# An eight-block fp32 kernel: one layer norm is spread among the parts of a product, gated products go in halves, and GpSimd takes copies and two of eight blocks

## The chip, the cores and the metric

One core of a Trainium2 chip runs the whole program in one launch. TensorE (PE) multiplies matrices into the eight banks of PSUM, VectorE (DVE) and ScalarE (ACT) read PSUM and SBUF, GpSimd (POOL) works on SBUF, SyncE (SP) issues most DMAs. The metric is device microseconds of one execution; the time before is the median of three runs.

## The reference, cut to what matters

The tensor x has 32 images of 16 x 16 points with 32 channels; read as tokens it is 32 sequences of 256. Eight residual blocks follow each other. The change is at the seam between the second (a spectral filter over tokens, "STU") and the third (a triangle product over the grid):

```
t = t + stu(ln(t))                       # spectral filter, by Fourier transform and short lags
n = ln_c(x)                              # the norm of the triangle block
a = sigmoid((n @ Wa1 + ba1) * (n @ Wa2 + ba2))
b = sigmoid((n @ Wb1 + bb1) * (n @ Wb2 + bb2))
g = sigmoid(n @ Wg + bg)
z = einsum('bikc,bkjc->bijc', a, b)      # 16 channels in a and b
x = x + g * (ln(z) @ Wz + bz)
```

## The kernel before, in words

All is float32, and every matmul shows as two instructions in the trace. The order of the work on each engine is written out by hand, with counting semaphores (`S(name)`, `wait_ge`, `then_inc`) between the engines; each engine works its own list strictly in order.

The tokens are kept in four quarters of 64. The late half of the tokens gets the filter's result by frequency products and a way back (`frequencies`, `way_back`, L889), and is ready first (`x_stu` at 1). The second quarter has a frequency product of its own on banks 4 to 7 (128 products of 64 x 32 weights), DVE turns it (`turn_products`, four transposes, L1644), PE takes it back (`way_back` on y_f2) and DVE adds it to quarter 1 (L1659). Quarter 0 gets its result as columns (`stu_cols`, added at L1656).

The norm of the triangle block (`LN_TRI`) goes quarter by quarter in the order 2, 3, 0, 1 (`TRI_ORDER`): PE subtracts the mean (`ln_centre`, L271), ACT squares (L370), PE spreads the mean square (`ln_spread`, L277), ACT takes Ln (L376) and Exp (L381), DVE multiplies (`normalise`, L1665). Before, DVE writes that product twice (`twice`): as columns `xm` in the arena, from which PE makes b and the gate, and as rows `xnH` (in the storage of xR), from which PE makes a.

Then PE makes the columns of a (`a_columns`) and of b, DVE adds the bias (`add_ab_bias`, L1681) and multiplies the two projections (L1695), and ACT takes the sigmoid (L1359 for a, L1371 for b). The matrix `a_bd` holds a eight times, each copy times a mask (`par16`): three blocks on ACT (`blocks_of_a`, L1362), five on DVE (L1700). When `a_bd` and `b_s` are there, PE makes z (L962). Most plain matmuls go through the helper `full`, L665, `keep_busy` among them: products whose result nobody reads.

Of the kernel before, what the change touches and what calls it, by code (L numbers as in the profile page):

```python
# [42 lines left out]
BUSY = {2: 2, 3: 6, 4: 1, 5: 1, 7: 0}  # L43
BUSY_ATTN, BUSY_TRI, BUSY_SCAN, BUSY_LOGITS = 4, (2, 2, 3, 1), 3, 2
BUSY_ROW, BUSY_START, BUSY_BACK = 1, 3, 1
# [3 lines left out]
BUSY_DRAIN = 1  # L49
ACT_BD, ACT_BD_FIRST = 3, 2  # L50
RES = 8
# [52 lines left out]
def build(nc, force_steps=False, **d):  # L104
    x, out = d["x"], d["out"]
    with ExitStack() as ctx:
# [155 lines left out]
        def var_bank(i):  # L262
            return [2, 4, 6, 4, 6, 6, 6, 6, 6][norm_of(i)] + i % 2

# [330 lines left out]
        def _(pool):  # L595
# [38 lines left out]


            def add_states(i):
                pool.wait_ge(S("x_early"), RES * (i + 1))
                pool.wait_ge(S("verdict"), i + 1)
                by_steps = pool.value_load(unsettled[0:1, i:i + 1], min_val=0, max_val=1)
                with pool.If(by_steps != 0):  # L640
                    pool.wait_ge(S("y_final"), i + 1)
                    for r in range(RES):
                        pool.tensor_tensor(*state_sum(i, r), ALU.add).then_inc(S(f"x_again{i}"), 1)
                        pool.wait_ge(S(f"x_again{i}"), r + 1)
# [16 lines left out]
        def _(pe):  # L661
# [212 lines left out]

            def frequencies(k0, rows, w):
                y_ps = bank[:, k0:k0 + 4, :].rearrange("p k n -> p (k n)")
                for n in range(FREQ // NQ):
                    for k in range(NQ):
                        f = FREQ // NQ * k + n
                        last = full(y_ps[C * k:C * k + C, 2 * C * n:2 * C * n + 2 * C], x_fb[rows, f, :],  # L880
                                    w[rows, f // FI, f % FI, :, :])
                last.then_inc(S("y_f_ps"), 1)

# [21 lines left out]

            pe.wait_ge(S("stu_rows"), 1)
            frequencies(4, slice(0, 2 * C), w_fr[1])

            pe.wait_ge(S("x_stu"), 1)
            for r in range(NQ):  # L910
                for q in range(NQ):
                    last = full(bank[C * q:C * q + C, 0, r * P:(r + 1) * P], ident[:, C * r:C * r + C],
                                r_stu.rearrange("p (n b) -> p n b", b=B)[:, :, G * q:G * q + G])
            last.then_inc(S("stu_cols"), 1)

            def centre_tri(p):
                pe.wait_ge(S("x_stu"), max(1, p))
                ln_centre(pe, ln_at(LN_TRI) + p, tokens(xQ, TRI_ORDER[p]))

            centre_tri(0)  # L920
            centre_tri(1)
            pe.wait_ge(S("y_f"), 8)
            way_back(y_f2, 0, range(G), 1, slice(T // 4, T // 2))
            ln_spread(pe, ln_at(LN_TRI))
            centre_tri(2)
            ln_spread(pe, ln_at(LN_TRI) + 1)

            def a_columns(ms):
                for m in ms:
# [3 lines left out]
                    if m % 8 == 7:  # L933
                        last.then_inc(S("ab_ps"), 1)

            pe.wait_ge(S("w_late_in"), 16)
            centre_tri(3)
            a_columns(range(8, 12))
            ln_spread(pe, ln_at(LN_TRI) + 2)
            a_columns(range(12, 16))  # L940
            ln_spread(pe, ln_at(LN_TRI) + 3)
            a_columns(range(0, 4))
            keep_busy(BUSY_TRI[0], 6)
            a_columns(range(4, 8))
            for m in range(16):
                last = full(bank[:, 4 + m // 4, (m % 4) * P:(m % 4 + 1) * P], xm[:, m * P:(m + 1) * P], wb)
# [7 lines left out]
            keep_busy(BUSY_TRI[1], 6)  # L954
            pe.wait_ge(S("a_bd"), 2)
            pe.wait_ge(S("b_s"), 1)
# [232 lines left out]
        def _(act):  # L1189
# [155 lines left out]
            ln_square(act, tri + 1)  # L1345
            ln_rstd(act, tri)
            ln_square(act, tri + 2)
            ln_rstd(act, tri + 1)
            ln_square(act, tri + 3)
            ln_rstd(act, tri + 2)  # L1350
            ln_rstd(act, tri + 3)
# [5 lines left out]
            sigmoids()  # L1357
            act.wait_ge(S("a_in"), 1)
            act.activation(a_s[:, :], a_in[:, :].rearrange("p (h m) -> p m h", h=16), ACT.Sigmoid).then_inc(S("a_s"), 1)  # L1359
            def blocks_of_a(gs):  # L1360
# [5 lines left out]
            act.wait_ge(S("a_s"), 1)  # L1366
            blocks_of_a(range(ACT_BD_FIRST))
            act.wait_ge(S("b_in"), 1)
# [4 lines left out]
            last.then_inc(S("b_s"), 1)  # L1373
            blocks_of_a(range(ACT_BD_FIRST, ACT_BD)).then_inc(S("a_bd"), 1)
            act.wait_ge(S("gate_ps"), 1)
# [118 lines left out]
        def _(dve):  # L1494
# [152 lines left out]
            for half in range(2):  # L1647
# [3 lines left out]
            last.then_inc(S("x_stu"), 1)  # L1651
            turn_products(1, y_f2)

            dve.wait_ge(S("stu_cols"), 1)
            x0 = tokens(xQ, 0).rearrange("p g (n r) -> p g n r", r=NQ)
            dve.tensor_tensor(x0, bank[:, 0, :].rearrange("p (r n g) -> p g n r", r=NQ, g=G), x0, ALU.add)\  # L1656
                .then_inc(S("x_stu"), 1)
            dve.wait_ge(S("back_f"), 3)
            dve.tensor_tensor(tokens(xQ, 1), by_batch(bank[:, 1, :]), tokens(xQ, 1), ALU.add).then_inc(S("x_stu"), 1)  # L1659

            def twice(j, i):

                h4 = xnH[:, 4 * j:4 * j + 4, :, :].rearrange("p h g w -> p g h w")
                for out_ in (xm.rearrange("p (w g h) -> p g h w", w=W, g=G)[:, :, 4 * j:4 * j + 4, :], h4):
                    last = dve.tensor_tensor(out_, bank[:, j, :].rearrange("p (g h w) -> p g h w", g=G, w=W),  # L1665
                                             rs[:, i % 2, :].rearrange("p (g h w) -> p g h w", g=G, w=W), ALU.mult)
                last.then_inc(S("ln_applied"), 1)

            def normalise(p):
                dve.wait_ge(S("ln_rstd"), ln_at(LN_TRI) + p + 1)  # L1670
                twice(TRI_ORDER[p], ln_at(LN_TRI) + p)

            normalise(0)
            normalise(1)
            normalise(2)
            pre4 = ab_pre.rearrange("p (m n) -> p m n", n=2 * CT)

            def add_ab_bias(k, half):
# [4 lines left out]
                                         ab_bias[:, k:k + 1, :].to_broadcast([P, 32, 2 * CT]), ALU.add)  # L1683

            dve.wait_ge(S("w_late_in"), 16)
            link(add_ab_bias(0, 1))
            normalise(3)
            for k in range(2):
                if k:
                    dve.wait_ge(S("a_in"), 1)  # L1690
                    link(add_ab_bias(1, 0))
                last = add_ab_bias(k, k)
                last.then_inc(S(["a_pre", "b_pre"][k]), 1)
                dve.wait_ge(S(["a_pre", "b_pre"][k]), 1)
                dve.tensor_tensor((b_in if k else a_in).rearrange("p (m c) -> p m c", c=CT), pre4[:, :, 0:CT], pre4[:, :, CT:2 * CT],  # L1695
                                  ALU.mult).then_inc(S(["a_in", "b_in"][k]), 1)

            dve.wait_ge(S("a_s"), 1)
            for g in range(ACT_BD, 8):
                last = dve.tensor_scalar(a_bd[:, :, g, :], a_s.rearrange("p (m i) -> p m i", i=16),  # L1700
# [333 lines left out]
```

## Time and profile before

| what | value |
|---|---|
| median of three runs | 379.24 us (376.47, 379.24, 379.54) |
| profiled execution, its own time | 377.4 us |
| span of its trace, first to last instruction | 374.0 us |
| mean granted TensorE clock | 0.989 of full speed |
| busy: PE, DVE, ACT, POOL | 341.5, 228.9, 190.7, 35.5 us |

The span is what the trace covers; 3.4 us of the execution's own time lie around it. Busy times of the engines overlap. A timeline row gives the start of an instruction or of several merged ones, the time from the first's start to the last's end, and in brackets how long the engine had been idle and what released it. "x256" counts instructions, two for each float32 matmul.

### The profile page before, as it was taken

To read this page: it belongs to the slowest core of one execution; us is meant where nothing else is said; L and a number is where in the kernel's file an instruction comes from. 1 tells how busy PE (TensorE), PEld (TensorE's weight loads), DVE (VectorE), ACT (ScalarE), POOL (GpSimd) and SP (SyncE) were. 2 spreads that over 40 slices of the span, in tenths; PEclk is the share of its full clock that TensorE was granted. 3 is DMA by queue.
4 is the path that set the end of the run, shared out by engine and by line. 5 is a ranking of instruction groups with operands and counts; after the bars stand their busy time and mean duration, and the time that the engine had idled before them with its cause. 6 is when DMAs were issued, how large, how long until landed. Compare 5 with 4: busy or idle time off the path is not lost.

```text
span 374.0 us, 9464 instructions
## 1 busy us (share of the span) xinstructions
PE 341.5 (91%) x4044; PEld 228.4 (61%) x4044; DVE 228.9 (61%) x461; ACT 190.7 (51%) x415; POOL 35.5 (9%) x38
## 2 busy tenths in 40 slices
PE   7969999999998999998889999799998899999890
PEld 2545666566646899956556379257646554773790
DVE  5679768689848403156956764643446476245894
ACT  2988688988868300044862656530346215033460
POOL 4027512122210001000000000000000000000000
PEclk9999999999999999999999999999999899999997
DMA  8960000000070000020000000000000000000004
GB/s 232 127 197 1 2 4 2 2 4 2 3 169 3 4 4 2 4 59 2 0 2 2 0 3 0 4 0 2 2 0 2 0 3 0 2 2 1 0 2 115
DMA packets 7426, 8.95 MB, mean 24 GB/s; under 512 B 3840, under 2 KB 6544, under 8 KB 7056
## 3 DMA queue, kind: packets, MB, share of 16 engines
q1 hardware_dynamic: 5718, 7.28, 9.1%
q10 hardware_dynamic: 1664, 1.05, 0.9%
q8 instruction: 33, 0.54, 0.6%
q14 instruction: 11, 0.09, 0.1%
HBM read 5.70 MB, written 1.05 MB: 18 GB/s over the span
## 4 chain that ended last, share of the span: by engine, by line
PE 64%; DVE 14%; ACT 10%; issue 5%; DMA 4%; SPq 2%; DVEq 0%; ACTq 0%
PE bank L665 30%; PE bank L1098 6%; PE bank L277 5%; PE bank L271 4%; DMA arena<-in_w_spec 4%; PE bank L1025 4%; PE bank L1036 3%; PE bank L865 2%; PE bank L889 2%; ACT lnv L376 2%; SPq L561 1%; ACT rs L381 1%; DVE arena L1796 1%; PE bank L778 1%; PE bank L1155 1%
## 5 line engine op out<-in xcount | busy, mean ns | idle before, releaser
L370 ACT ACTIVATE sq<-bank 128x512 f32<-128x512 f32 x33 | 19.4, 591 | 64.1 <-PE bank L271 50.4
L665 PE MATMUL bank<-xn,sb_w_attn 128*128 128x512 f32 x64 | 34.5, 621 | 3.7 <-ACT attn_scratch L1233 1.9
L665 PE MATMUL bank<-sb_consts 128*128 128x512 f32 (+1 forms) x80 | 35.4, 553 | 0.0
L277 PE MATMUL bank<-sq,sb_consts 128*128 128x512 f32 x66 | 34.7, 611 | 0.5 <-ACT sq L370 0.2
L376 ACT ACTIVATE lnv<-bank 128x512 f32<-128x512 f32 x33 | 19.7, 596 | 30.2 <-PE bank L277 29.9
L1098 PEld LDWEIGHTS bank<-arena,sb_w_late 128*128 128x128 f32 x180 | 23.0, 190 | 10.9 <-DVE arena L1854 8.0
L665 PE MATMUL bank<-arena 64*32 64x256 f32 (+4 forms) x466 | 26.6, 381 | 2.5 <-ACT arena L1266 1.2
L1098 PE MATMUL bank<-arena,sb_w_late 128*128 128x128 f32 (+1 forms) x180 | 26.4, 283 | 1.5 <-DVE arena L1854 0.3
L611 POOL TENSOR_TENSOR attn_scratch<-attn_scratch 128x512 f32<-128x512 f32 x16 | 20.4, 1275 | 72.1 <-DVE attn_scratch L1567 72.1
L1036 PE MATMUL bank<-arena,sb_w_late 128*128 128x128 f32 x136 | 26.3, 277 | 0.0
L1025 PE MATMUL bank<-arena,sb_consts 128*128 128x128 f32 x136 | 26.1, 276 | 0.1
L665 PEld LDWEIGHTS bank<-arena 64*32 64x32 f32 (+3 forms) x466 | 17.2, 167 | 14.5 <-issue 6.7
L1406 ACT ACTIVATE arena<-bank 128x128 f32<-128x128 f32 x68 | 18.8, 277 | 13.3 <-PE bank L1036 13.1
L665 PE MATMUL bank<-arena,attn_scratch 128*32 128x128 f32 (+2 forms) x768 | 23.9, 293 | 0.6 <-DVE attn_scratch L1609 0.6
L1854 DVE SCALAR_TENSOR_TENSOR arena<-bank,xn 128x128 f32<-128x128 f32 x30 | 8.7, 290 | 25.5 <-PE bank L1098 25.1
L665 PEld LDWEIGHTS bank<-arena,attn_scratch 128*32 128x32 f32 (+1 forms) x768 | 22.7, 129 | 1.9 <-DVE attn_scratch L1609 0.8
L271 PE MATMUL bank<-xQ,sb_consts 128*128 128x512 f32 x40 | 20.9, 613 | 1.0 <-DMA sb_consts<-in_consts 0.6
L1025 PEld LDWEIGHTS bank<-arena,sb_consts 128*128 128x128 f32 x136 | 20.5, 192 | 1.7 <-issue 1.7
L381 ACT ACTIVATE rs<-lnv 128x512 f32<-128x512 f32 x33 | 20.8, 630 | 1.0
L1036 PEld LDWEIGHTS bank<-arena,sb_w_late 128*128 128x128 f32 x136 | 20.6, 192 | 0.2
L665 PEld LDWEIGHTS bank<-sb_consts 128*128 128x128 f32 x80 | 14.2, 197 | 10.8 <-issue 10.6
L665 PEld LDWEIGHTS bank<-wvo,xn 128*128 128x128 f32 x128 | 15.9, 191 | 6.2 <-issue 6.2
(208 smaller groups left out, 625.3 us busy)
## 6 DMA issues: line engine op xcount, KB each, us to landing
sb_w_late<-in_w_late SPq DMA_DIRECT2D x1, 1100.5 KB, 18.6
arena<-in_w_spec SPq DMA_DIRECT2D x4, 256.0 KB
arena<-arena SPq DMA_DIRECT2D x4, 256.0 KB, 4.1
arena<-fourier SPq DMA_DIRECT2D x1, 768.0 KB, 16.4
sb_w_attn<-in_w_attn SPq DMA_DIRECT2D x1, 641.0 KB, 8.2
xR<-in_x ACTq DMA_DIRECT2D x4, 128.0 KB, 3.1
xR<-in_x SPq DMA_DIRECT2D x4, 128.0 KB, 4.1
arena<-arena SPq DMA_DIRECT2D x4, 128.0 KB, 2.3
```

Of the source, the lines that this page charges most:

```text
L271: pe.matmul(bank[:, centre_bank(i), :], centre, src, start=True, stop=True).then_inc(S("ln_centred"), 1)
L277: pe.matmul(bank[:, var_bank(i), :], mean32, sq[:, i % 2, :], start=True, stop=True)\
L370: act.activation(sq[:, i % 2, :], bank[:, centre_bank(i), :], ACT.Square).then_inc(S("ln_squared"), 1)
L376: act.activation(lnv[:, i % 2, :], bank[:, var_bank(i), :], ACT.Ln, bias=LN_EPS[norm_of(i)])\
L381: act.activation(rs[:, i % 2, :], lnv[:, i % 2, :], ACT.Exp, scale=-0.5).then_inc(S("ln_rstd"), 1)
L611: link(pool.tensor_tensor(qn[:, u % QN, :], qe[:, u % 2, :], qn[:, u % QN, :], ALU.mult))
L665: return mm(ps, lhsT, rhs, start=True, stop=True)
L1025: mm(place(s, h), ident, z_[:, h, s % RES, :, :], start=True, stop=False)
L1036: mm(place(s_, h), rvt[i], before(h, s_ % RES), start=False, stop=True)\
L1098: last = mm(bank[:, 4 + h % 2, B * lo:B * hi], band[i][:, w, :], carry[:, h - 1, w + lo:w + hi, :], start=(w == 1), stop=(w == 2), skip_gr ...
L1406: act.activation(y_[:, h, s_ % RES, 1:PASS + 1, :], bank[:, 4 + h + 2 * (s_ % 2), 0:PASS * HALF].rearrange("p (n g) -> p n g", g=HALF), AC ...
L1854: dve.scalar_tensor_tensor(out=carry[:, h, 1:5, :], in0=bank[:, 4 + h % 2, 0:P].rearrange("p (w b) -> p w b", b=B), scalar=0.0, in1=xn[:, ...
```

## The change

PE: the second quarter's 128 frequency products are cut into four parts; the centring and spreading of quarters 2 and 3, and the product for quarter 0's columns, stand between the parts. The way back of the second quarter comes after the columns of a for quarters 2 and 3, in bank 6 and no longer in bank 1. The spread of the norm uses banks 1, 0, 1, 4. One of two idle products ahead of the last columns of a is dropped. The products for b wait for POOL's copies.

DVE: quarters 2 and 3 are normalised ahead of the transposes, once each (rows only). The gated products of a and b are made in halves. DVE makes four of the eight blocks of `a_bd`.

POOL: copies each normalised quarter from rows to columns, and makes two blocks of `a_bd`.

ACT: the square of quarter 0 comes after the Exp of quarter 3; the sigmoid of a goes in two halves; two blocks of `a_bd` in place of three, both ahead of the sigmoid of b.

```diff
-BUSY_ATTN, BUSY_TRI, BUSY_SCAN, BUSY_LOGITS = 4, (2, 2, 3, 1), 3, 2
+BUSY_ATTN, BUSY_TRI, BUSY_SCAN, BUSY_LOGITS = 4, (1, 2, 3, 1), 3, 2
...
-ACT_BD, ACT_BD_FIRST = 3, 2
+ACT_BD, POOL_BD = 2, 2
...
         def var_bank(i):
-            return [2, 4, 6, 4, 6, 6, 6, 6, 6][norm_of(i)] + i % 2
+            k = norm_of(i)
+            if k == LN_TRI:
+                return [1, 0, 1, 4][i - ln_at(k)]
+            return [2, 4, 6, None, 6, 6, 6, 6, 6][k] + i % 2
...
# gpsimd, behind the zeroing of b_s
+            for p in range(CH):
+                rows = slice(4 * TRI_ORDER[p], 4 * TRI_ORDER[p] + 4)
+                pool.wait_ge(S("ln_applied"), ln_at(LN_TRI) + p + 1)
+                pool.tensor_copy(xm.rearrange("p (w g h) -> p g h w", w=W, g=G)[:, :, rows, :],
+                                 xnH[:, rows, :, :].rearrange("p h g w -> p g h w")).then_inc(S("xm_in"), 1)
+            pool.wait_ge(S("a_s"), 1)
+            for g in range(8 - POOL_BD, 8):
+                last = pool.tensor_scalar(a_bd[:, :, g, :], a_s.rearrange("p (m i) -> p m i", i=16), par16[:, g:g + 1],
+                                          None, ALU.mult)
+            last.then_inc(S("a_bd"), 1)
...
# tensor
             pe.wait_ge(S("stu_rows"), 1)
-            frequencies(4, slice(0, 2 * C), w_fr[1])
-            ...                               # stu_cols, as in stu_columns() below
-            centre_tri(0)
-            centre_tri(1)
-            pe.wait_ge(S("y_f"), 8)
-            way_back(y_f2, 0, range(G), 1, slice(T // 4, T // 2))
-            ln_spread(pe, ln_at(LN_TRI))
-            centre_tri(2)
-            ln_spread(pe, ln_at(LN_TRI) + 1)
+            second_quarter(0)
+            centre_tri(0)
+            centre_tri(1)
+            second_quarter(1)
+            ln_spread(pe, ln_at(LN_TRI))
+            ln_spread(pe, ln_at(LN_TRI) + 1)
+            second_quarter(2)
+            stu_columns()                     # waits for ln_logged of quarter 3
+            second_quarter(3)
+            centre_tri(2)
             pe.wait_ge(S("w_late_in"), 16)
-            centre_tri(3)
             a_columns(range(8, 12))
             ln_spread(pe, ln_at(LN_TRI) + 2)
             a_columns(range(12, 16))
+            pe.wait_ge(S("y_f"), 8)
+            way_back(y_f2, 0, range(G), 6, slice(T // 4, T // 2))
+            pe.wait_ge(S("ln_logged"), ln_at(LN_TRI) + 3)
+            centre_tri(3)
+            a_columns(range(0, 2))
             ln_spread(pe, ln_at(LN_TRI) + 3)
-            a_columns(range(0, 4))
+            a_columns(range(2, 4))
             keep_busy(BUSY_TRI[0], 6)
             a_columns(range(4, 8))
+            pe.wait_ge(S("xm_in"), CH)
             for m in range(16):
...
-            pe.wait_ge(S("a_bd"), 2)
+            pe.wait_ge(S("a_bd"), 3)
...
# scalar
+            for half in (1, 0):
+                act.wait_ge(S("a_in"), 2 - half)
+                last = act.activation(a_s.rearrange("p (m h) -> p m h", h=16)[:, :, 8 * half:8 * half + 8],
+                                      a_in[:, 512 * half:512 * half + 512].rearrange("p (h m) -> p m h", h=8), ACT.Sigmoid)
+            last.then_inc(S("a_s"), 1)
...
# vector
-            turn_products(1, y_f2)
+            normalise(0)                      # rows only
+            normalise(1)
             dve.wait_ge(S("stu_cols"), 1)
...
+            turn_products(1, y_f2)
...
             link(add_ab_bias(0, 1))
+            ab_product(0, 1).then_inc(S("a_in"), 1)
+            normalise(2)
+            dve.wait_ge(S("back_f"), 3)
+            dve.tensor_tensor(tokens(xQ, 1), by_batch(bank[:, 6, :]), tokens(xQ, 1), ALU.add).then_inc(S("x_stu"), 1)
             normalise(3)
+            add_ab_bias(0, 0).then_inc(S("a_pre"), 1)
+            dve.wait_ge(S("a_pre"), 1)
+            ab_product(0, 0).then_inc(S("a_in"), 1)
+            dve.wait_ge(S("a_in"), 2)
+            link(add_ab_bias(1, 0))
+            ab_product(1, 0)
+            add_ab_bias(1, 1).then_inc(S("b_pre"), 1)
+            dve.wait_ge(S("b_pre"), 1)
+            ab_product(1, 1).then_inc(S("b_in"), 1)

             dve.wait_ge(S("a_s"), 1)
-            for g in range(ACT_BD, 8):
+            for g in range(ACT_BD, 8 - POOL_BD):
```

## Rows read from the trace of the kernel before

**Rows 1.** Windows: stretch, length, busy PE, PEld, DVE, ACT, POOL, granted clock, DMA share, GB/s.

```profile
150.00:165.00 15.00, 15.00 (x423) 12.81 (x424) 4.47 (x7) 1.21 (x2) 0.00 (x0) 1.00 0.02 4
165.00:176.00 11.00, 9.46 (x42) 5.16 (x41) 7.36 (x9) 7.13 (x11) 0.00 (x0) 1.00 0.24 48
```

**Rows 2.** Timeline, 149 to 167 us: start, length, instruction, [idle before <-releaser].

```profile
149.87 8.17 PE L665 MATMUL bank<-arena,attn_scratch 64*32 64x64 f32 x256
150.00 0.69 DVE L1650 TENSOR_TENSOR xQ<-bank,xQ 128x512 f32<-128x512 f32 x1 [1.06 <-PE bank L889]
...
158.98 1.98 PE L271 MATMUL bank<-xQ,sb_consts 128*128 128x512 f32 x4
...
160.90 3.10 PE L889 MATMUL bank<-arena,attn_scratch 128*32 128x64 f32 x128
...
163.93 1.13 PE L277 MATMUL bank<-sq,sb_consts 128*128 128x512 f32 x2
164.05 1.21 SPq L561 DMA_DIRECT2D arena<-in_w  x3
164.06 0.69 DVE L1659 TENSOR_TENSOR xQ<-bank,xQ 128x512 f32<-128x512 f32 x1 [2.84 <-PE bank L889]
...
165.09 0.60 ACT L376 ACTIVATE lnv<-bank 128x512 f32<-128x512 f32 x1 [3.48 <-PE bank L277]
...
165.72 0.63 ACT L381 ACTIVATE rs<-lnv 128x512 f32<-128x512 f32 x1
```

**Rows 3.** Timeline, 175 to 188 us.

```profile
175.66 1.16 PE L665 MATMUL bank<-sb_w_late,xR 128*128 128x128 f32 x8
...
176.66 3.74 PE L665 MATMUL bank<-sb_w_late,arena 128*128 128x128 f32 x32
176.86 1.22 DVE L1681 TENSOR_TENSOR arena<-bank,sb_w_late 128x1024 f32<-128x1024 f32 x1 [1.25 <-PE bank L665]
...
179.38 2.02 ACT L1359 ACTIVATE arena<-arena 128x1024 f32<-128x1024 f32 x1 [5.01 <-DVE arena L1695]
...
180.23 3.60 PE L665 MATMUL bank<-arena,sb_w_late 128*128 128x512 f32 x8
...
181.43 2.19 ACT L1362 ACTIVATE arena<-arena,sb_consts 128x1024 f32<-128x1024 f32 x2
...
181.89 1.23 DVE L1695 TENSOR_TENSOR arena<-arena 128x1024 f32<-128x1024 f32 x1
...
183.03 3.40 DVE L1700 TENSOR_SCALAR arena<-arena,sb_consts 128x1024 f32<-128x1024 f32 x5
...
183.52 2.11 ACT L1371 ACTIVATE arena<-arena 128x512 f32<-128x512 f32 x2
...
186.73 3.77 PE L962 MATMUL bank<-arena 128*32 128x128 f32 x128 [1.18 <-ACT arena L1362]
```

**Rows 4.** Groups by line and shape, DVE, 145 to 200 us: busy us, mean ns.

```profile
L1665 DVE TENSOR_TENSOR arena<-bank,rs 128x512 f32<-128x512 f32 x4 | 4.2, 1040 | 3.5 <-ACT rs L381 3.5
...
L1665 DVE TENSOR_TENSOR xR<-bank,rs 128x512 f32<-128x512 f32 x4 | 2.7, 671 | 0.0
L1644 DVE STREAM_TRANSPOSE attn_scratch<-bank 128x512 f32<-128x512 f32 x4 | 2.5, 684 | 7.4 <-PE bank L665 7.4
```

**Rows 5.** Groups by line and shape, POOL, whole span.

```profile
L611 POOL TENSOR_TENSOR attn_scratch<-attn_scratch 128x512 f32<-128x512 f32 x16 | 20.4, 1275 | 72.1 <-DVE attn_scratch L1567 72.1
L625 POOL TENSOR_TENSOR arena<-arena 128x1024 f32<-128x1024 f32 x3 | 7.1, 2361 | 0.5 <-POOL attn_scratch L611 0.5
...
L619 POOL TENSOR_SCALAR sb_w_stu<-sb_w_stu,sig 128x128 f32<-128x128 f32 x1 | 0.6, 620 | 0.2 <-POOL attn_scratch L611 0.2
```

**Rows 6.** Timeline, 1.7 to 5.8 us, POOL and DVE.

```profile
1.74 3.52 POOL L607 MEMSET arena<- 128x4096 f32 x1 [0.15 <-POOL arena L605]
...
4.54 0.73 DVE L1511 TENSOR_SCALAR fw<-fw 128x4 f32<-128x4 f32 x1
...
5.51 0.23 DVE L1513 TENSOR_SCALAR fw<-fw 128x4 f32<-128x4 f32 x1
```

## What the change is predicted to do

> **What bounds the kernel now.** After the page I read the chain of waits through the seam between the filter and the triangle block, then the windows there, then the timeline row by row. The windows say that the seam has two halves of different kind. From 150 to 165 us PE is busy all the time, at the full 2.4 GHz level (granted clock 1.00) [rows 1]: it works through the second quarter's product, the first centrings and the way back without a hole [rows 2]. From 165 us on no engine is full (PE 9.46, DVE 7.36, ACT 7.13 of 11 us) [rows 1]: here the end is set by a relay, and its last part is what the reader should follow [rows 3]: last columns of a (175.66), bias on DVE (176.86), product, sigmoid on ACT (179.38 to 181.40), two blocks of a_bd, sigmoid of b, a third block on ACT, and only then z on PE at 186.73, released by that third ACT block. What the change is worth is how much earlier z starts; behind z nothing is edited, so that difference goes to the end undiminished.
>
> **The front: what moves.** The second quarter's 256 instructions take 8.17 us [rows 2], 2.04 for each of the four parts, from 149.87. The add that the centring waits for ends at 150.69 [rows 2], so nothing waits at 151.9, and PE stays the bound. I add up PE's list. Four instructions of centring take 1.98 with the tail, some 0.43 each in the stream; the product and the columns of quarter 0 together end where centring starts, 9.11 after 149.87, so the columns cost about 1.0 [rows 2]. Eight instructions of a's columns cost 1.00 (176.66 - 175.66) [rows 3]. The way back costs 3.03 (163.93 - 160.90) [rows 2]. Cutting the product makes PE go five more times from one shape of weights to another; I take 0.1 for each, worked out from that 1.0 for 32 short instructions, bounds 0 and 0.3. Sum: 149.87 + 8.17 + four products of 0.86 + 1.0 + 0.96 (centre quarter 0) + 1.0 + 0.96 + 1.0 + 3.03 + 0.5 = 170.0 for the end of the way back, which was 163.93.
>
> Covered on the way, at nothing: squares, Ln and Exp of quarters 2 and 3, finished at about 160 beside the third part of the product (Ln starts 1.16 after its spread, Ln and Exp take 1.26 [rows 2]); the products for quarter 0's columns wait for that Ln, which is about 0.8 us early; behind that new wait on PE stand the fourth part and all the rest. The transposes (2.5 [rows 4]) run from 163.1 to 165.7 and are due at 166.9. DVE's half bias, half product and normalise(2) end at about 169.7, due at 170.1: the thinnest cover, and if it is gone each tenth goes to the end. The SP queue waits for back_f at 3, so its three loads of the expert weights leave at about 170 and not at 164.05 [rows 2]; the experts are two layers on, which is time enough.
>
> Behind the way back the relay of quarter 1: add 0.69, centre and square, spread, Ln and Exp 1.26, normalise 0.67 [rows 2, 4]. With the lags of the rows: add 170.13 to 170.82, square 172.04 to 172.63, spread 172.7, Ln 173.84, Exp to 175.10, normalise to 175.80, last columns of a at 175.85. Before they started at 175.66 [rows 3]. **So the front, for all its moving, gives -0.2 to +0.3: nothing.** What it took away (four writes of 1.04 us into the columns, on DVE [rows 4]) was on the path, and the longer PE list takes its place.
>
> **The back: what gets shorter.** Bias at 177.05 (the same lag of 1.20), 1.22 long; the product of one half, about 0.65 (half of 1.23, and some start); the sigmoid of one half, about 1.1 (half of 2.02, and some start) [rows 3]: a_s at 180.1 and not 181.40. Gain here 1.3.
> On b: POOL's fourth copy starts at 175.85. The trace shows no such copy; bounds are 0.5 (a memset at 3.52 per 4096 elements [rows 6] has only writes) and 1.28 (two inputs, 512 elements [rows 5]), with up to half as much again for the scattered write, as DVE shows (1.04 against 0.67 [rows 4]). I take 0.8, near the memset: at most one read. It ends at 176.7, PE's a columns at 176.85, so it is hidden; at 2.0 it would cost 1.0. Products for b 176.85 to 180.42, the gate's and the idle ones to 185.8 (3.57, 3.60 and 1.8 by instruction count [rows 3]).
> DVE: bias of b 179.0 to 180.2, product half to 180.9, bias to 182.15, product half to 182.85 (183.12 before). ACT: two blocks 180.1 to 182.3, sigmoid of b 182.9 to 185.0, and no third block. DVE: four blocks of 0.68 (3.40/5 [rows 3]).
> POOL: two blocks of 1024 elements behind a_s. Nearest rows: 0.62 for a tensor_scalar of 128 elements, and two-input tensor_tensors of 1.28 and 2.36 for 512 and 1024, 2.12 ns an element [rows 5]. A memset's 0.86 ns an element [rows 6] and one input of two (1.06 ns) give 1.4 and 1.6 for a block; the 128-element row scaled by 8 gives 5.0. I take 1.5: POOL from 180.2 to 183.2.
>
> **Where the two meet.** One early pair of rows decides how I let POOL and DVE overlap: a DVE tensor_scalar of four elements, which takes 0.23 alone, takes 0.73 when it starts inside POOL's long memset, and ends at 5.27, 0.01 after the memset's end at 5.26 [rows 6]. So DVE's blocks, which are tensor_scalars at 0.66 ns an element (the tensor_tensor of as many needs 1.20 [rows 3]), will not run beside POOL's: they wait from 182.85 to 183.2 and end at 185.9. z starts at 186.0, with PE itself ready at 185.8. **Sum: 186.73 - 186.0 = 0.7 us saved.** Without that meeting z would start at PE's 185.8.
> The Trainium skill (SBUF — State Buffer, Who interferes with whom) calls this an exclusive lock on a port pair that DVE's two-port modes share with GpSimd, and the trace agrees for tensor_scalar (0.73 against 0.23). The same section goes further and says that a DVE instruction with two SBUF inputs also contends with a GpSimd one that reads SBUF; no row here shows or denies that, and it would turn the sign of the sum: the second rival.
>
> **The rivals.** (1) POOL and DVE don't disturb each other in these shapes, and POOL is quick: z at PE's 185.8, a gain of 0.9 to 1.0. For it: only one instruction shows the wait. Against: it shows it to 0.01 us.
> (2) Slower: the half products of b (two SBUF inputs) also wait for POOL's blocks, and POOL's for them. Place: 180.2, where POOL begins and the first half product is ready at nearly the same time. Then everything with the port stands in one line: block 180.2 to 181.7, product to 182.35, block to 183.85 (the second bias beside it), product to 184.5, four blocks to 187.2, z at 187.3: 0.55 later than before. It decides from POOL blocks of about 1.2 us up; each 0.1 on a block costs 0.2, so 2.36 would make it 2.3 us.
> (3) POOL's block is far dearer than 1.5: at 5.0 POOL ends at 190.2, DVE's blocks at 192.9, z 6.2 late. The 128-element row allows it, the longer rows speak against it.
> (4) PE's clock falls in a new hole. PE would idle 1.2 us at most here; before, it stood 1.18 us ahead of z [rows 3] and kept 1.00.
> That the change doesn't do what it says has little room: each moved step has its own wait.
>
> **How the numbers follow.** The profiled execution took 377.4 us on its own clock, so the forecast by its rows is 376.7; rival 1 gives 376.4, rival 2 377.95 (to 379.7), rival 3 up to 383.6. The runs shown are 376.47, 377.4, 379.24 and 379.54: the profiled one is 1.8 below the median, and four draws spread over 3 us, so about 1% is what a measurement of this kernel can tell from no change. The new time will be such a draw; I set the sum on the mean of the four, 378.2: 377.5 for the forecast, 377.2 to 377.3 for rival 1, 378.7 for rival 2. Chances: forecast 0.38, rival 2 0.32, rival 1 0.18, rival 3 in some degree 0.08, the clock 0.04. Range: rival 1 with a low draw (2 below) 375.0; rival 2 with a high draw (1.5 above) 380.3. Faster by over 1% has no case but a misread front, 0.04; slower by over 1% needs rival 3 at its full size or the clock, 0.06; within 1% 0.90.
>
> **What would show each step.** Last columns of a at 175.5 to 176.2 (front right); the end of the half sigmoid near 180.1; xm copies under 1.0 and never the last release of b's products; POOL's blocks near 1.5 with b's two half products at 0.65 (forecast) or with a start or length drawn out to a POOL block's end (rival 2); the first of DVE's four blocks ending later than 0.7 after its start (the meeting); z released by DVE, near 186.0. The prediction is wrong if the spread of quarter 1 or the copies release PE much later than this, if POOL's blocks pass 2 us, or if the clock in 165 to 190 is not 1.00.

## The result, and the profile after

The changed kernel took 380.91 us in the median (378.76 to 384.19), the kernel before 379.11 beside it: a ratio of 1.0059, 95% interval 1.0038 to 1.0079. A second set of the same kernel gave 1.0028 (1.0004 to 1.0051). So it is slower, by 0.3 to 0.6%, where 377.5 us, 0.7 less than the mean of the runs then known, was forecast. The profiled execution took 380.7 us, 3.3 more than that of before. Its page:

```profile
span 377.8 us, 9462 instructions
PE 344.9 (91%) x4042; PEld 229.8 (61%) x4042; DVE 227.5 (60%) x458; ACT 190.3 (50%) x415; POOL 46.4 (12%) x44
```

DVE lost 1.4 us, POOL gained 10.9. What matters is the seam, in the timeline of after:

```profile
149.09 2.17 PE L680 MATMUL bank<-arena,attn_scratch 64*32 64x64 f32 x64
...
169.30 0.69 DVE L1717 TENSOR_TENSOR xQ<-bank,xQ 128x512 f32<-128x512 f32 x1 [0.46 <-PE bank L905]
...
175.12 1.16 PE L680 MATMUL bank<-sb_w_late,xR 128*128 128x128 f32 x8 [0.77 <-DVE xR L1686]
175.13 1.09 POOL L642 COPY arena<-xR 128x512 f32<-128x512 f32 x1 [5.17 <-DVE xR L1686]
...
176.26 3.65 PEld L680 LDWEIGHTS bank<-sb_w_late,arena 128*128 128x128 f32 x32 [0.18 <-POOL arena L642]
...
178.30 1.11 ACT L1388 ACTIVATE arena<-arena 128x512 f32<-128x512 f32 x1 [1.54 <-DVE arena L1709]
179.51 6.54 POOL L646 TENSOR_SCALAR arena<-arena,sb_consts 128x1024 f32<-128x1024 f32 x2 [3.30 <-ACT arena L1388]
179.68 1.49 DVE L1709 TENSOR_TENSOR arena<-arena 128x512 f32<-128x512 f32 x1
...
182.34 0.72 DVE L1709 TENSOR_TENSOR arena<-arena 128x512 f32<-128x512 f32 x1
182.98 4.27 DVE L1731 TENSOR_SCALAR arena<-arena,sb_consts 128x1024 f32<-128x1024 f32 x4
...
187.31 5.44 PE L990 MATMUL bank<-arena 128*32 128x128 f32 x128 [2.06 <-DVE arena L1731]
```

The second quarter's product (t0) begins between 149.0 and 151.5 in the profiles of this study, at 149.87 before [rows 2], and nothing ahead of it was edited; so every time of the seam is counted from t0. The reader sees three things. The last columns of a start 26.03 behind t0, before 25.79 [rows 3]: the front gave nothing. The second half of a's sigmoid ends at 179.41, 30.32 behind t0, before 31.53: the halves paid 1.2. Then that is lost again and more: POOL's two blocks take 6.54, beside them DVE's first half product takes 1.49 and its four blocks 4.27, and z starts 38.22 behind t0 and not 36.86 [rows 2, 3]: **1.36 us late**, 0.36% of the time. Here z also took 5.44 for 3.77. The windows (columns: stretch, length, PE, PEld, DVE, ACT, POOL busy with counts, granted clock, DMA share, GB/s) say why:

```profile
186.00:187.00 1.00, 0.00 (x0) 0.00 (x0) 1.00 (x2) 1.00 (x1) 0.06 (x1) 1.00 0.00 0
187.00:188.00 1.00, 0.69 (x20) 0.66 (x24) 0.26 (x1) 0.06 (x1) 0.00 (x0) 0.83 0.00 0
188.00:189.00 1.00, 1.00 (x26) 0.96 (x25) 0.00 (x0) 0.00 (x0) 0.00 (x0) 0.50 0.00 0
...
190.00:191.00 1.00, 1.00 (x28) 0.96 (x23) 0.00 (x0) 0.22 (x1) 0.00 (x0) 0.50 0.00 0
191.00:192.00 1.00, 1.00 (x42) 1.00 (x37) 0.00 (x0) 0.98 (x2) 0.00 (x0) 0.97 0.06 16
```

PE had idled 2.06 us (a hole of 2.06, in what follows), and the granted clock went to 0.50, the 1.2 GHz level, for some 3 us. At the end of z the profiled execution is -0.78 (t0) + 1.36 + 1.67 = 2.25 behind that of before. A further 1.0 comes between z's end and a late centring (338.83 before, 342.08 after), a stretch in which the clock read 0.95 from 225 to 260 us and 1.00 before. The single profiles of the kernels below show 0.95 or 1.00 in that stretch, 0.95 also in the fastest; I don't lay it on the change.

### The profile page after: what moved, and what is told of

It is laid out like the page before. It is cut to its first block, busy times and chain, and to the rows that moved or that the text cites. A ratio compares the mean times of both kernels' runs of the same rounds, so it can differ in the third digit from the quotient of the medians.

```text
span 377.8 us, 9462 instructions
## 1 busy us (share of the span) xinstructions
PE 344.9 (91%) x4042; PEld 229.8 (61%) x4042; DVE 227.5 (60%) x458; ACT 190.3 (50%) x415; POOL 46.4 (12%) x44
## 4 chain that ended last, share of the span: by engine, by line
PE 69%; DVE 16%; ACT 9%; issue 4%; DMA 1%; SPq 0%; DVEq 0%; ACTq 0%
PE bank L680 31%; PE bank L280 7%; PE bank L1126 6%; PE bank L274 6%; PE bank L1053 4%; PE bank L1064 3%; PE bank L880 2%; PE bank L905 2%; ACT lnv L379 2%; PE bank L990 1%; ACT rs L384 1%; DMA sb_consts<-in_consts 1%; DVE arena L1827 1%; PE bank L781 1%; DVE arena L1731 1%
## 5 line engine op out<-in xcount | busy, mean ns | idle before, releaser
L1126 PEld LDWEIGHTS bank<-arena,sb_w_late 128*128 128x128 f32 x180 | 23.0, 190 | 10.9 <-DVE arena L1885 8.0
L665 POOL MEMSET arena<- 128x128 f32 x4 | 0.8, 206 | 155.3 <-DVE xQ L1873 131.8
```

The costliest lines, as they stand in the source:

```text
L1126: last = mm(bank[:, 4 + h % 2, B * lo:B * hi], band[i][:, w, :], carry[:, h - 1, w + lo:w + hi, :], start=(w == 1), stop=(w == 2), skip_gr ...
```

## The experiments

After the result I held one theory, that POOL's two blocks, by their own length and by what they do to DVE, make z late; and one rival, that the clock's fall behind the hole ahead of z is the loss. Later a third question came up: where the gain of the copies went. No kernel leaves any of the computation out. Ratios are to the kernel before on the same chip, with 95% intervals; "z" is its start counted from the t0 of the same trace.

| kernel | t0, us | z from t0, us | z long, us | ratio |
|---|---|---|---|---|
| before | 149.87 | 36.86 | 3.77 | |
| the changed kernel | 149.09 | 38.22 | 5.44 | 1.0059 (1.0038 to 1.0079) |
| the same again (e12) | 150.81 | 38.21 | 3.77 | 1.0028 (1.0004 to 1.0051) |
| e1: no POOL blocks, six on DVE | 150.28 | 37.13 | 3.77 | 1.0028 (1.0003 to 1.0052) |
| e3: one POOL block | 149.49 | 37.29 | 3.77 | 1.0006 (0.9983 to 1.0029) |
| e9: no POOL blocks, ACT three | 150.74 | 36.52 | 3.77 | 0.9992 (0.9965 to 1.0018) |
| e10: e9 with DVE's columns | 151.45 | 37.66 | 3.77 | 1.0027 (0.9996 to 1.0057) |
| e5: POOL's blocks kept apart | 150.21 | 41.51 | 3.77 | profiled only, 384.05 us |
| e2: hole filled | 151.21 | 38.17 | 3.77 | 1.0016 (0.9994 to 1.0037) |
| e4: before with POOL's blocks | 149.11 | 38.16 | 3.77 | 1.0076 (1.0049 to 1.0104) |
| e7: e4, hole filled | 149.04 | 38.16 | 3.77 | 0.9988 (0.9971 to 1.0004) |
| e8: before, one idle product more | 151.01 | 36.87 | 3.77 | 1.0017 (0.9993 to 1.0041) |
| e6: before with the halves | 151.29 | 36.18 | 3.77 | 0.9970 (0.9953 to 0.9986) |
| e11: e6 with POOL's copies | 149.10 | 34.32 | 3.77 | 0.9900 (0.9869 to 0.9932) |

**e1_no_pool_blocks.** The changed kernel without POOL's blocks; DVE makes six.

```diff
-ACT_BD, POOL_BD = 2, 2
+ACT_BD, POOL_BD = 2, 0
-            pool.wait_ge(S("a_s"), 1)      # and the loop of two tensor_scalars
-            pe.wait_ge(S("a_bd"), 3)
+            pe.wait_ge(S("a_bd"), 2)
```

> The changed kernel without POOL's two blocks: POOL still copies the columns, DVE makes six blocks. Theory A (POOL's two blocks are the loss: 2.85 and 3.72 us long, they draw out DVE's product to 1.49 and its four blocks to 4.27, and the hole that this leaves on PE lets the clock fall in z): the product takes 0.69, six blocks about 4.1, z starts 37.2 to 37.4 us after the second quarter's product and not 38.2, the granted clock in z is 1.00 and z takes 3.8: 2.5 us below the changed kernel, so within 0.5 us of the kernel before. Rival C (the loss is in the new order of the norm and in POOL's copies): it stays 1.5 us or more above the kernel before.

z came at 37.13, 1.09 earlier than with POOL's blocks. Its timeline:

```profile
180.83 0.69 DVE L1704 TENSOR_TENSOR arena<-arena 128x512 f32<-128x512 f32 x1
...
183.30 4.06 DVE L1726 TENSOR_SCALAR arena<-arena,sb_consts 128x1024 f32<-128x1024 f32 x6
187.41 3.77 PE L985 MATMUL bank<-arena 128*32 128x128 f32 x128 [1.01 <-DVE arena L1726]
```

Without POOL beside it DVE's half product takes 0.69 for 1.49, and six blocks take 4.06, less than four took (4.27). The ratio did not follow as far as z did: by z it should be 1.0007, its interval begins at 1.0003 and its middle is 1.0028, which the second set of the changed kernel has too. So the time expected here, within 0.5 us of the kernel before, was missed. The span of the trace is on record for every execution: in the mean it is 1.56 us longer than that of the kernel before, of which z is 0.27 and the granted clock, 0.0019 lower, by the estimate given under e12 some 0.6; 0.7 stays open. That POOL's blocks make z late is shown; that the whole time comes back without them is not.

**e3_one_pool_block.** One block on POOL, five on DVE.

```diff
-ACT_BD, POOL_BD = 2, 2
+ACT_BD, POOL_BD = 2, 1
```

> The changed kernel with one block on POOL and five on DVE. Theory A with a wait that lasts only while POOL has a block: POOL is done at about 33.4 us after the second quarter's product, ahead of DVE's blocks, which take 3.4; the first half product still takes 1.49; z starts at 37.4 to 37.7, with the clock at 1.00: 2 to 2.5 below the changed kernel. If POOL's block costs by its length alone, the same; if what counts is that POOL runs beside DVE at all, half of the 1.36 us by which z is late stays.

```profile
179.90 2.85 POOL L646 TENSOR_SCALAR arena<-arena,sb_consts 128x1024 f32<-128x1024 f32 x1 [3.30 <-ACT arena L1388]
180.07 1.49 DVE L1709 TENSOR_TENSOR arena<-arena 128x512 f32<-128x512 f32 x1
...
183.33 3.40 DVE L1731 TENSOR_SCALAR arena<-arena,sb_consts 128x1024 f32<-128x1024 f32 x5
186.78 3.77 PE L990 MATMUL bank<-arena 128*32 128x128 f32 x128 [1.14 <-DVE arena L1731]
```

The first block still draws the half product out to 1.49, by 0.80. POOL has ended (182.75) when DVE's blocks begin, and five of them take 3.40, as they did before [rows 3]. So the second block costs 0.93 (38.22 - 37.29), nearly all of it on DVE's blocks (4.27 - 3.40).

**e5_pool_alone.** POOL's blocks end before DVE's products of b begin, so each is seen by itself.

```diff
-            last.then_inc(S("a_bd"), 1)      # POOL
+            last.then_inc(S("pool_bd"), 1)
...
             link(add_ab_bias(1, 0))
+            dve.wait_ge(S("pool_bd"), 1)
             ab_product(1, 0)
```

> The changed kernel, but DVE waits with b's first half product, and so with all behind it, until POOL's two blocks are done: their length with nothing on DVE beside them. If POOL's block is dear by itself (the sum's 1.5 was mis-sized): both blocks 2.8 to 2.9, together 5.7, and b's half products 0.69. If the wait for DVE makes them dear: 2.0 to 2.1 each or less (0.8 us less than 2.85, the time by which DVE's product was drawn out). z starts about 4 us later than in the changed kernel either way.

By line (durations in ns: least, median, most), first the kernel after, then e5:

```profile
L646 POOL TENSOR_SCALAR arena<-arena,sb_consts x2: 2851/3284/3717, 179.5 to 182.3; 128x1024 f32<-128x1024 f32 x2
L1731 DVE TENSOR_SCALAR arena<-arena,sb_consts x4: 734/1126/1520, 183.0 to 186.5; 128x1024 f32<-128x1024 f32 x4
```

```profile
L646 POOL TENSOR_SCALAR arena<-arena,sb_consts x2: 2844/2847/2850, 180.6 to 183.4; 128x1024 f32<-128x1024 f32 x2
```

And the timeline of e5:

```profile
186.40 0.69 DVE L1710 TENSOR_TENSOR arena<-arena 128x512 f32<-128x512 f32 x1 [5.63 <-POOL arena L646]
188.28 3.51 PE L680 MATMUL bank<-sb_consts 128*128 128x512 f32 x4 [3.63 <-DVE arena L1704]
188.87 2.74 DVE L1733 TENSOR_SCALAR arena<-arena,sb_consts 128x1024 f32<-128x1024 f32 x4
191.72 3.77 PE L991 MATMUL bank<-arena 128*32 128x128 f32 x128
```

Alone, a POOL block is 2.85 us and four DVE blocks are 2.74. Beside each other POOL's second block is 3.72 and DVE's four 4.27, in turn 1.52, 0.74, 1.51, 0.73. None of DVE's waits until POOL's instruction ends (186.05 in the kernel after). POOL's first block kept its 2.85 and drew out the half product that began 0.17 after it. The second half product, which began together with POOL's second block at 182.34, took only 0.72; there the POOL block grew, beside this product and DVE's first three blocks. What decides which side pays was not tried. The idle products show the clock again: four instructions in 3.51 behind a hole of 3.63, with the granted clock at 0.50 from 188 to 191 us, and in 1.88 elsewhere.

**e2_hole_filled.** Two more idle products ahead of z in the changed kernel; everything else stays.

```diff
-BUSY_ATTN, BUSY_TRI, BUSY_SCAN, BUSY_LOGITS = 4, (1, 2, 3, 1), 3, 2
+BUSY_ATTN, BUSY_TRI, BUSY_SCAN, BUSY_LOGITS = 4, (1, 4, 3, 1), 3, 2
```

> The changed kernel with four idle products in place of two ahead of z, 1.7 us more of them, which end before z can start. Theory A: z still starts at 38.2 us after the second quarter's product, but the granted clock stays 1.00 and z takes 3.8 in place of 5.4: 1.7 us below the changed kernel, 0.3 to 1.0 above the kernel before. Rival B (the clock falls for another reason than the 2.06 us hole ahead of z): z takes 5.4 as before and the time is that of the changed kernel, 2.2 above the kernel before.

```profile
185.44 3.60 PE L680 MATMUL bank<-sb_consts 128*128 128x512 f32 x8
...
189.38 3.77 PE L990 MATMUL bank<-arena 128*32 128x128 f32 x128 [0.34 <-DVE arena L1731]
```

The hole is 0.34, z is 3.77 long and as late as ever (38.17). The ratio is 1.0016: z's late start alone would make 1.0035. What is missing does not lie at the seam, as e7 shows.

**e4_before_pool_blocks.** The kernel before, with POOL making two of DVE's five blocks and nothing else of the change.

```diff
+            pool.wait_ge(S("a_s"), 1)
+            for g in range(8 - POOL_BD, 8):
+                last = pool.tensor_scalar(a_bd[:, :, g, :], a_s.rearrange("p (m i) -> p m i", i=16), par16[:, g:g + 1],
+                                          None, ALU.mult)
+            last.then_inc(S("a_bd"), 1)
...
-            for g in range(ACT_BD, 8):
+            for g in range(ACT_BD, 8 - POOL_BD):
```

> The kernel before with only one part of the change: POOL makes two of DVE's five blocks. Theory A: POOL runs from 31.6 us after the second quarter's product to 37.5 or later and releases z at 37.6 to 38.3 in place of 36.86; the hole on PE ahead of z is over 2 us, the clock falls and z takes over 5 us: 1.5 to 3 us above the kernel before. Rival C: no loss, within 0.5 us of the kernel before.

```profile
180.75 6.46 POOL L637 TENSOR_SCALAR arena<-arena,sb_consts 128x1024 f32<-128x1024 f32 x2 [34.06 <-ACT arena L1364]
181.14 1.79 DVE L1700 TENSOR_TENSOR arena<-arena 128x1024 f32<-128x1024 f32 x1
182.86 3.46 DVE L1705 TENSOR_SCALAR arena<-arena,sb_consts 128x1024 f32<-128x1024 f32 x3
187.27 3.77 PE L967 MATMUL bank<-arena 128*32 128x128 f32 x128 [2.47 <-POOL arena L637]
```

This one edit, that should unload DVE, makes z 1.30 later, with POOL itself the last to come. The product of full size is drawn out from 1.23 [rows 3] to 1.79, three blocks take what five took. The hole of 2.47 left the clock at 1.00 in the profiled execution, where I had expected z at over 5 us: such a hole need not make it fall. The ratio, 1.0076, is 2.9 us, of which z explains 1.30.

**e7_before_pool_blocks_filled** and **e8_before_filled** ask what filling that hole is worth, and whether one more idle product does anything for the kernel before, which has a hole of 1.18 [rows 3].

```diff
# e7: e4 with
+BUSY_ATTN, BUSY_TRI, BUSY_SCAN, BUSY_LOGITS = 4, (2, 4, 3, 1), 3, 2
# e8: before with
+BUSY_ATTN, BUSY_TRI, BUSY_SCAN, BUSY_LOGITS = 4, (2, 3, 3, 1), 3, 2
```

> The kernel before with POOL's two blocks, and four idle products in place of two ahead of z. That kernel without the fill was 2.9 us above before, of which 1.3 is z's later start, though in the one profiled execution the clock stayed 1.00 behind a hole of 2.47 us. If the rest is the clock falling in many of the timed executions: z starts at 38.2 as without the fill and the time falls to 1.0 to 1.8 above before. If the rest has another cause: it stays at 2.5 to 3.3.

> The kernel before with three idle products in place of two ahead of z, which end at about 36.4, ahead of z at 36.86: a control for the fill. If the fill helps only where the hole is long: the same time as before, within 0.5 us. If the clock falls in the kernel before too in some executions, or if idle products help anywhere: 0.5 to 1.5 us below.

```profile
187.20 3.77 PE L967 MATMUL bank<-arena 128*32 128x128 f32 x128 [0.74 <-POOL arena L637]
```

e7 has z where e4 has it (38.16, hole 0.74), and measures 0.9988 against 1.0076; e8 measures 1.0017, no gain. That e7 comes out no slower than before, with z 1.3 us later, has its reason outside the seam. In the mean e7's span is 1.18 us longer than that of the kernel before beside it, which agrees with z's 1.30; but only 1.84 us of its time lie outside the span, against 3.65. e2 is the same case: its span is 2.36 longer, with 1.82 outside against 3.62, and its mean span, 377.44, lies between those of the two sets of the changed kernel, 378.15 and 377.24. e8 has 1.61 outside, and its span is 2.67 longer without any delay of z; the clock, 0.0034 lower, is some 1.2 of that by the estimate under e12, the rest stays open. So the ratio of a kernel with more idle products doesn't show what they do at the seam. By spans the hole of e4 does cost something: 2.10 longer over its six executions, 0.9 more than e7, and its mean granted clock, 0.9820 against 0.9845, is an estimated 0.9 us of that. Why less time lies outside the span with more idle products, no run here shows.

**e6_halves_only.** The kernel before with a's and b's gated products and a's sigmoid in halves.

```diff
-                dve.tensor_tensor((b_in if k else a_in).rearrange("p (m c) -> p m c", c=CT), pre4[:, :, 0:CT], pre4[:, :, CT:2 * CT],
-                                  ALU.mult).then_inc(S(["a_in", "b_in"][k]), 1)
+            ab_product(0, 1).then_inc(S("a_in"), 1)
+            add_ab_bias(0, 0).then_inc(S("a_pre"), 1)
+            dve.wait_ge(S("a_pre"), 1)
+            ab_product(0, 0).then_inc(S("a_in"), 1)
+            ...                               # the same for b, and two half sigmoids on ACT
```

> The kernel before with only the gated products in halves (products and a's sigmoid; DVE keeps writing the columns, no work on POOL, order of PE as before). If the halves are the part that gains: a_s 1.2 to 1.4 us earlier than before (30.1 to 30.3 after the second quarter's product, before 31.5), DVE's five blocks end at 36.2 and z starts at 36.2 and not 36.86: 0.6 us below the kernel before, 2.5 or more below the changed kernel. If b's columns or PE hold it, z starts at 36.8 and the time is that of before.

```profile
180.29 1.12 ACT L1360 ACTIVATE arena<-arena 128x512 f32<-128x512 f32 x1 [1.50 <-DVE arena L1690]
...
184.02 3.40 DVE L1709 TENSOR_SCALAR arena<-arena,sb_consts 128x1024 f32<-128x1024 f32 x5
187.47 3.77 PE L962 MATMUL bank<-arena 128*32 128x128 f32 x128 [0.48 <-DVE arena L1709]
```

The sigmoid ends 30.12 behind t0, 1.4 earlier; z gains 0.68, since DVE's five blocks behind b's second product become the last to come. The ratio, 0.9970, is a gain of 1.1 us (0.5 to 1.8), which agrees.

**e9, e10, e11: the order against the copies.** e9 is e1 with the third block back on ACT behind b's sigmoid, so it has the new order, the halves and the copies. e10 is e9 with the columns written by DVE again. e11 is e6, in the old order, with POOL's copies, and one idle product fewer ahead of the last columns of a, as in the change. e9 and e11 thus differ in the order of the lists of PE, DVE and ACT, and in the PSUM banks that go with it.

```diff
# e9: e1 with
-ACT_BD, POOL_BD = 2, 0
+ACT_BD, POOL_BD = 3, 0
-            blocks_of_a(range(ACT_BD)).then_inc(S("a_bd"), 1)
+            blocks_of_a(range(2))
...
+            blocks_of_a(range(2, ACT_BD)).then_inc(S("a_bd"), 1)      # behind b's sigmoid
# e10: e9 with
-                pool.tensor_copy(xm.rearrange("p (w g h) -> p g h w", w=W, g=G)[:, :, rows, :], ...
+                dve.tensor_tensor(xm.rearrange("p (w g h) -> p g h w", w=W, g=G)[:, :, 4 * j:4 * j + 4, :], ...
# e11: e6 with
+BUSY_ATTN, BUSY_TRI, BUSY_SCAN, BUSY_LOGITS = 4, (1, 2, 3, 1), 3, 2
+                pool.tensor_copy(xm.rearrange("p (w g h) -> p g h w", w=W, g=G)[:, :, rows, :], ...
+            pe.wait_ge(S("xm_in"), CH)
-                for out_ in (xm.rearrange("p (w g h) -> p g h w", w=W, g=G)[:, :, 4 * j:4 * j + 4, :], h4):
+                for out_ in (h4,):
```

> The changed kernel with a_bd made as before (two blocks on ACT, one more behind b's sigmoid, five on DVE) and none on POOL: what stays of the change is the new order on PE, the halves and POOL's copies. If the halves are what gains and the new order with the copies gains nothing (last columns of a at 26.0 against 25.8 us after the second quarter's product, b's columns 0.35 later): z starts at 36.4 to 36.6 against 36.2 for the halves alone and 36.86 before; 0.3 us below before. If the new order does carry a gain: z at 36.0 or earlier, and below the kernel with the halves alone.

> The kernel of the run above, but DVE writes the columns itself behind each row product and POOL does nothing: it prices POOL's copies in the new order. If they take writes off the path (as the prediction had it): the last columns of a start 1.5 to 1.7 us later (26.0 to 27.6), z at 37.6 to 38.1, 1 to 2 us slower than the run above. If the new order had made those writes harmless: no later than 0.3 us.

> The kernel before with the halves and with POOL's copies, PE's order as before (one idle product in place of two ahead of the last columns of a, no block on POOL). In the old order DVE's writes of 1.04 us stand between Exp and the columns of a in every quarter. If they are on the path there, taking them off moves the last columns of a from 25.8 to 23.7 to 24.3 us after the second quarter's product, and z from 36.2 to 34.2 to 34.8: 2.0 to 2.7 us below the kernel before, faster than both. If the copies only move the wait to POOL, or the new order was needed for them: 36.0 to 36.2, the time of the halves alone.

The timeline of e11:

```profile
149.10 3.18 PE L671 MATMUL bank<-arena,attn_scratch 64*32 64x64 f32 x93
...
163.29 0.69 DVE L1669 TENSOR_TENSOR xQ<-bank,xQ 128x512 f32<-128x512 f32 x1 [2.87 <-PE bank L895]
...
172.42 0.68 DVE L1697 TENSOR_TENSOR arena<-arena 128x512 f32<-128x512 f32 x1
...
172.55 1.16 PE L671 MATMUL bank<-sb_w_late,xR 128*128 128x128 f32 x8
172.56 1.47 POOL L638 COPY arena<-xR 128x512 f32<-128x512 f32 x1 [0.75 <-DVE xR L1675]
...
183.42 3.77 PE L969 MATMUL bank<-arena 128*32 128x128 f32 x128 [0.35 <-DVE arena L1716]
```

and of e9 and e10:

```profile
176.77 1.16 PE L675 MATMUL bank<-sb_w_late,xR 128*128 128x128 f32 x8 [0.77 <-DVE xR L1682]
...
187.26 3.77 PE L985 MATMUL bank<-arena 128*32 128x128 f32 x128 [0.35 <-DVE arena L1727]
```

```profile
177.68 1.00 DVE L1679 TENSOR_TENSOR arena<-bank,rs 128x512 f32<-128x512 f32 x1
...
178.74 1.16 PE L670 MATMUL bank<-sb_w_late,xR 128*128 128x128 f32 x8 [1.69 <-DVE arena L1679]
...
189.11 3.77 PE L979 MATMUL bank<-arena 128*32 128x128 f32 x128 [0.48 <-DVE arena L1724]
```

In the old order quarter 1 is added 14.2 behind t0 (163.29 - 149.10; before 14.2 too [rows 2]), in the new order 20.2 (169.30 - 149.09). e11's last columns of a start 23.45 behind t0, e9's 26.03, e10's 27.29, and z follows: 34.32, 36.52, 37.66. **The copies are worth 1.14 us in the new order and 1.86 in the old (there together with dropping one idle product, not tried apart); the new order costs 2.20.** In e10 PE waits 1.69 for DVE's write of the columns, which the products for a don't read: the signal stands behind it. What a signal behind the rows alone would give, without POOL, was not tried. e11, the old order with halves and copies and without POOL's blocks, beats both kernels: 375.86 us, ratio 0.9900 (0.9869 to 0.9932), of which z explains 2.54 us, 0.67%. Its span is 2.74 shorter in the mean, and 1.0 less lies outside the span (2.76 against 3.78).

**e12_changed_again** is the changed kernel, to see whether the clock falls in each execution.

> The changed kernel itself, profiled once more beside the kernel before: does the clock fall ahead of z as a rule, or did the one profiled execution happen on it? If the 2.06 us hole makes it fall in most executions: z takes 5 to 5.5 us again, and the mean granted clock of its runs lies about 0.004 below that of the kernel before. If it falls only now and then: z takes 3.8 here, and the clocks of the runs lie between.

```profile
189.02 3.77 PE L990 MATMUL bank<-arena 128*32 128x128 f32 x128 [2.07 <-DVE arena L1731]
```

The same hole to 0.01, z as late (38.21), and the clock stayed at 1.00. In this set the two kernels have the same mean granted clock, 0.9835, and the changed kernel's span is 1.52 us longer in the mean (377.24 against 375.72): z's 1.35, and 0.2. Outside the span it has 3.04 against 3.52, which leaves 1.04, the 0.28% measured. In the first set its mean clock is 0.9804; the kernel before, whose clocks are not on record there, has 0.9844 over the 104 executions of the other sets. An estimate: with PE busy for 345 us, 0.01 of clock is some 3.4 us, so 0.004 is 1.4. With z's 1.36, and 0.5 to 0.8 less outside the span, that makes 2.0 to 2.2 us; measured are 2.2 (0.59% of 379.1). The difference between the sets is thus the clock.

Whether the hole ahead of z is what lowers it is not settled. A mean clock of 0.980 or less came in 13 of 29 executions of the changed kernel and 3 of 6 of e4, against 5 of 104 of the kernel before; but also in 4 of 12 of e1 and 3 of 12 of e2, whose holes are 1.01 and 0.34.

## Why the prediction was wrong, step by step

**Right: the front.** Last columns of a were set at 25.98 behind t0 and came at 26.03. That what it took from DVE was on the path and a longer PE list takes its place is what e9, e10 and e11 show, with a price that I did not see: 2.2 us at z. The relay of quarter 1 (add, centre, square, spread, Ln, Exp, normalise) stands bare behind six more microseconds of PE's list.

**Right: the halves.** a_s was set at 30.23 and ended at 30.32.

**A little off: the copies.** Taken at 0.8, measured at 1.06 to 1.09, between the stated bounds. "Never the last release" of b's products was wrong: b's columns wait 0.18 for POOL.

**The step that failed: POOL's block, "I take 1.5".** It takes 2.85 alone and 3.72 beside DVE's blocks. I took the slope of a memset and half of a two-input instruction [rows 5, 6]; the row of the same operation, 0.62 for 128 elements [rows 5], was the better guide, though not when scaled by 8: from 128 to 1024 elements the slope is (2.85 - 0.62)/896, 2.5 ns an element, more than the two-input tensor_tensor's 2.36 us for 1024 [rows 5]. The Trainium skill (GPSIMD Engine Reference, 4.1 Engine selection) has one-input elementwise work roughly at line rate on GpSimd. For this form the runs don't bear that out: 2.85 (e5) against DVE's 0.68. The price alone turns the forecast's sign: by its own rule, DVE's blocks behind POOL's end, two blocks of 2.85 end at 185.9 in its times and z starts at 188.7, 2.0 late and not 0.7 early.

**Mis-sized with it: the meeting.** I let four DVE blocks wait 0.35 for POOL's end, and b's half products nothing. Measured, b's first half product is 0.80 longer and DVE's blocks 1.53 longer (4.27 against 2.74). With 0.1 of lags and copies DVE comes to its blocks 0.91 later than set, and spends on them 4.27 in place of 3.07: together 2.1, the whole of 38.22 against 36.13. It was my second rival's place, its instruction and its sign; but its rule, one instruction at a time to the end, is not what the rows show (the second half product took 0.72 beside POOL), and with 2.85 a block it would have given 3.25 us (0.55 and 0.2 for each 0.1 beyond 1.5), not 1.36. The Trainium skill (SBUF — State Buffer, Who interferes with whom) says that a DVE instruction with two SBUF inputs contends with a GpSimd one that reads SBUF: e1 and e3 show that (0.69 against 1.49). The same section has the loser blocked for the whole instruction, which it says of DVE's two-port modes. Here nothing shows that: POOL's block was 2.85 and the product's delay 0.80, and DVE's tensor_scalars took 1.52 at most beside a block of 3.72.

**Wrong in its number: the clock.** "PE would idle 1.2 us at most": it idled 2.06, since the blocks ended later. I gave the fall 0.04; it came in one of the two profiled executions of this kernel. It isn't the cause of z's start, and e4 and e12 show that it needn't follow. And the difference at z did not go to the end "undiminished": in e12 the span kept it, but 0.5 us less lay outside the span, for a reason that no run shows.

At z the whole can be split along a chain of kernels, each compared with the one before it: 36.86 before, -0.68 for the halves (e6), -1.86 for the copies (e11), +2.20 for the new order (e9), +1.70 for the new split of the blocks, which makes 38.22 by construction. Of the 1.70, 1.09 are POOL's two blocks against DVE's (e1) and 0.61 the third block taken from ACT (e9 to e1). With e9's split the change would have been even within its interval (0.9992).

## What to carry to other kernels

Price an operation on an engine by a row of the same operation with the same kind of operands, and let a single row that disagrees with the convenient ones widen the sum, not only a rival's chance. When work is moved to a helper engine, ask first which instructions of the engine it relieves will run beside it: here two blocks taken from DVE made DVE's rest as long as before or longer. And try the parts of a change apart: the halves and the copies were worth 2.5 us at z in the old order, and the new order of the norm ate the gain. Where a record gives both the time and the span of the trace, compare both.

## What the runs showed of the hardware that was not expected

A tensor_scalar with a mask per partition takes POOL 2.85 us for 128x1024 float32, DVE 0.68 as one of five in a row. Beside it a DVE product of two SBUF operands of 512 elements takes 1.49 for 0.69 and one of 1024 takes 1.79 for 1.23; DVE's tensor_scalars take 1.52 and 0.73 in turn. Early in the kernel a small one ended 0.01 after a memset [rows 6]; here none ended with a POOL block. A half product that began together with a POOL block took 0.72. It goes the other way too: POOL's copy takes 1.47 beside DVE's half product (e11), 1.06 to 1.09 elsewhere, and its block 3.72 for 2.85. Behind holes of nearly the same length the clock fell once (2.06) and stayed twice (2.07 and 2.47). And the time outside the span is a kernel's own: 3.5 to 3.8 us before, 3.0 for the changed kernel, 1.6 to 1.8 with more idle products.
